# Graph layer with 512 columns: 16 gathered tiles per block and a loop of single tiles in place of 17 gathered tiles

## The reference

```
def _gin_conv(h, src, dst, w, b, eps, n_nodes):
    agg = jax.ops.segment_sum(h[src], dst, num_segments=n_nodes)
    return ((1.0 + eps) * h + agg) @ w + b
...
h = jax.nn.relu(_gin_conv(x, src, dst, w1, b1, eps1, n))
h = jax.nn.relu(_gin_conv(h, src, dst, w2, b2, eps2, n))
return _gin_conv(h, src, dst, w3, b3, eps3, n)
```

## Time and profile before

| | us |
|---|---|
| median of 3 runs | 4946.31 (4939.7 to 4948.61) |
| the profiled execution, its time | 4950.88 |
| the profiled execution, span from first to last instruction | 4949.2 |
| of it: attention layer with its gathers, about 622 to 1980 | 1358 |
| first graph layer, about 2340 to 3130 | 790 |
| 512-wide layer, about 3130 to 4335 | 1205 |
| last graph layer, about 4335 to 4949 | 614 |

### The profile page before, as it was taken

The page is one execution under the profiler, slowest core; times in us unless marked ns, Lnnn a source line. Parts: engine busy times, 40 slices in busy tenths (PEclk is TensorE's granted clock), DMA queues, the critical chain, the costliest instruction groups (busy, mean ns, idle before and its releaser), DMA issues. The chain is left out here.

```text
span 4949.2 us, 70593 instructions
## 1 busy us (share of the span) xinstructions
PE 3788.6 (77%) x15851; PEld 2474.8 (50%) x15852; DVE 2212.0 (45%) x7809; ACT 1419.7 (29%) x2721; POOL 2665.5 (54%) x4165
## 2 busy tenths in 40 slices
PE   3886645555555555885899999688888888879999
PEld 1233334444444444775677777344444444467777
DVE  6996756666666666345111121222222223222222
ACT  3982222222222222235344444100000010033333
POOL 6780066666666665013544444366666666655554
PEclk9999967777777777985999999899999999899999
DMA  4442133333333333026767666477777676656665
GB/s 137 174 190 68 55 93 90 88 92 92 93 89 93 93 93 81 0 59 176 200 186 203 190 183 180 148 207 212 207 210 209 206 213 204 183 167 188 200 183 170
DMA packets 347068, 730.73 MB, mean 148 GB/s; under 512 B 77999, under 2 KB 171821, under 8 KB 342577
## 3 DMA queue, kind: packets, MB, share of 16 engines
q0 software_dynamic: 176144, 461.72, 33.3%
q10 hardware_dynamic: 100802, 157.63, 10.2%
q1 hardware_dynamic: 69980, 109.80, 6.5%
HBM read 622.28 MB, written 106.64 MB: 147 GB/s over the span
## 5 line engine op out<-in xcount | busy, mean ns | idle before, releaser
L901 POOL DMA_INDIRECT a_gathered<-table,record x850 | 807.2, 950 | 688.0 <-issue 368.3
L2265 POOL DMA_INDIRECT l_gathered<-table,record x782 | 760.5, 972 | 478.2 <-issue 275.5
L2455 PE MATMUL bank<-l_gathered,l_onehot 128*125 128x512 f32 x1564 | 774.8, 649 | 189.5 <-DMA l_gathered<-table,record 108.0
L1829 POOL DMA_INDIRECT l_gathered<-table,record x578 | 546.6, 946 | 487.8 <-PE bank L2037 218.4
L1250 PE MATMUL bank<-a_gathered,a_onehot 128*125 128x264 f32 x1700 | 564.4, 490 | 101.0 <-DVE a_gathered L1054 85.6
L2455 PEld LDWEIGHTS bank<-l_gathered,l_onehot 128*125 128x125 f32 x1564 | 312.5, 205 | 629.8 <-issue 464.7
L1943 ACT ACTIVATE l_part<-l_packed 128x1000 fp32r<-128x1000 bf16 (+1 forms) x396 | 411.6, 1070 | 578.6 <-DMA l_packed<-adjacency 176.6
L1250 PEld LDWEIGHTS bank<-a_gathered,a_onehot 128*125 128x125 f32 x1700 | 389.3, 241 | 201.9 <-issue 67.5
L2018 PE MATMUL bank<-rows_last,l_part 125*125 125x512 f32 x1650 | 407.4, 404 | 35.1 <-ACT l_part L1943 22.4
L2018 PE MATMUL bank<-rows_first,l_part 125*125 125x512 f32 x1650 | 407.3, 406 | 35.1 <-ACT l_part L1943 35.1
L2018 PEld LDWEIGHTS bank<-rows_first,l_part 125*125 125x125 f32 x1650 | 309.0, 188 | 127.1 <-issue 44.6
(11 more groups left out here) (282 smaller groups left out, 5613.4 us busy)
## 6 DMA issues: line engine op xcount, KB each, us to landing
l_packed<-adjacency ACTq DMA_DIRECT2D x264, 250.0 KB
adjacency<-d_stage SPq DMA_DIRECT2D x33, 1562.5 KB
l_packed<-adjacency ACTq DMA_DIRECT2D x132, 281.2 KB
l_gathered<-table,record POOLq DMA_INDIRECT x1360
a_gathered<-table,record POOLq DMA_INDIRECT x850
table<-rows_first POOLq DMA_DIRECT2D x50, 250.0 KB, 3.4
table<-l_work ACTq DMA_DIRECT2D x50, 250.0 KB
l_source_rows<-table ACTq DMA_DIRECT2D x50, 250.0 KB
```

Source lines behind the costliest of these rows:

```text
L901: pool.indirect_dma_start(out=gathered0[s][:, j * TW:(j + 1) * TW], out_offset=None, in_=table0, in_offset=bass.IndirectOffsetOnAxis(ap=re ...
L1829: pool.indirect_dma_start(out=gathered[g][:, j, :], out_offset=None, in_=table, in_offset=bass.IndirectOffsetOnAxis(ap=record[k.t][:, j, 0 ...
L2265: pool.indirect_dma_start(out=gathered[:, j * w:(j + 1) * w], out_offset=None, in_=table, in_offset=bass.IndirectOffsetOnAxis(ap=record[t] ...
L2455: last = pe.matmul(total[0:NB, 0:w], onehot[t][:, j, :], rows[:, j, :], start=False, stop=(j == T - 1), skip_group_check=True)
```

## The change

A gathered block's first 2048 edges are now one fixed round of 16 tiles (`WT` = 16, `RW` = 2048), without a loop around it: record loads, gathers, one-hots and matmuls are plain code, and their waits count by the place in the order (`round_of`, `filled_of`). Edges from `rest_from[b]` = min(first_edge[b] + 2048, first_edge[b+1]) up to the block's end are single tiles of 128 edges, in a loop `Fori(lo, hi, P)` that usually runs no time. It is the loop that the tabled blocks already had, with a step of 128 in place of 32, and now serves both kinds. Its records are loaded by GpSimd (`gather_rest`) instead of SP. VectorE does its part of that loop at the end of the step (`onehot_rest`). PE starts the sum with its first tile instead of a matmul with zeros, and reads the bounds of the loop after the 16 tiles. Three small VectorE operations at the layer's start make `rest_from`, and GpSimd and PE wait for them.

The diff, cut to its core:

```
+WT = 16
+RW = WT * P
...
-                QUARTERS = [(0, 4), (4, 8), (8, 12), (12, T)]
+                QUARTERS = [(0, 4), (4, 8), (8, 12), (12, WT)]
...
-                onehot = tiles("onehot", [P, T, NB])
-                gathered = phase.enter_context(nc.sbuf_tensor(f"l{n}_gathered", [P, T * w], F32))[:, :]
+                onehot = tiles("onehot", [P, WT, NB])
+                gathered = phase.enter_context(nc.sbuf_tensor(f"l{n}_gathered", [P, WT * w], F32))[:, :]
...
+                def round_of(s, i):
+
+                    if isinstance(i, int) and i >= PAIRS - TABLED:
+                        return (PAIRS - TABLED) + (i - (PAIRS - TABLED)) // 2
+                    return i
+
+                def filled_of(s, i):
+
+                    if isinstance(i, int) and i >= PAIRS - TABLED:
+                        return 2 * (PAIRS - TABLED) + (i - (PAIRS - TABLED))
+                    return 2 * i + s
...
-                        ends = [first_edge[0:1, bass.ds(b + e, 1)] for e in range(2)]
+                        ends = [rest_from[0:1, bass.ds(b, 1)], first_edge[0:1, bass.ds(b + 1, 1)]]
...
+                def load_records(engine, s, i):
+                    if tabled(s, i):
+                        return
+                    t, r = record_of(s, i), round_of(s, i)
+                    lo = engine.value_load(first_edge[0:1, bass.ds(block_at(s, i), 1)], min_val=0, max_val=E)
+                    engine.wait_ge(round_gathered[t], r + 1)
+                    engine.dma_start(record[t][:, 0:WT, :].rearrange("p j c -> p (j c)"),
+                                     edges[bass.ds(lo, RW), :].rearrange("(p j) c -> p (j c)", j=WT)).then_inc(record_loaded[t], 16)
...
-                    def gather_few(lo, hi):
-                        with pool.Fori(lo, hi, OV) as at:
+                    def gather_rest():
+                        lo, hi = [pool.snap(reg, min_val=0, max_val=E) for reg in bounds]
+                        with pool.Fori(lo, hi, P) as at:
                             before = few_of(pool, few)
+                            wait_apart(pool, few_used, before + 1, 1)
+                            pool.dma_start(few_record[:, :], edges[bass.ds(at, P), :]).then_inc(few_loaded, 16)
                             wait_apart(pool, few_loaded, before * 16 + 16, 16)
                             pool.indirect_dma_start(
...
-                        with pool.Fori(lo, hi, RE) as at:
-                            wait_apart(pool, record_loaded[t], count_of(pool, rounds[t]) * 16 + 16, 16)
-                            before = count_of(pool, filled)
-                            for q, (j0, j1) in enumerate(QUARTERS):
...
+                        wait_apart(pool, record_loaded[t], round_of(s, i) * 16 + 16, 16)
+                        for q, (j0, j1) in enumerate(QUARTERS):
+
+                            wait_apart(pool, quarters_used, filled_of(s, i) * NQ + q + 1, 1)
+                            for j in range(j0, j1):
...
+                        gather_rest()
                         keep(found)
...
+                    dve.tensor_copy(first_f[:, :], first_edge[:, :]).then_inc(rest_steps, 1)
...
+                    dve.scalar_tensor_tensor(rest_f[:, :], first_f[:, 0:BLOCKS], float(RW), first_f[:, 1:BLOCKS + 1],
+                                             ALU.add, ALU.min).then_inc(rest_steps, 1)
...
+                    dve.tensor_copy(rest_from[:, :], rest_f[:, :]).then_inc(rest_ready, 1)
...
-                    over_steps(dve, [(rounds_of, 0), (finish, 1), (halve, 4)], split_source, 6, AHEAD + 1)
+                    over_steps(dve, [(onehots, 0), (finish, 1), (halve, 4), (onehot_rest, 0)], split_source, 6, AHEAD + 1)
...
-                            pe.matmul(total[0:NB, 0:w], zeros[:, 0:NB], zeros[:, 0:w], start=True, stop=True)
...
+                                    last = pe.matmul(total[0:NB, 0:w], onehot[t][:, j, :], rows[:, j, :], start=(j == 0),
+                                                     stop=False, skip_group_check=True)
...
+                        lo, hi = rest_range(pe, s, i)
+                        with pe.Fori(lo, hi, P) as at:
+                            before = few_of(pe, few)
+                            pe.wait_ge(few_ready, before + 1)
+                            pe.wait_ge(few_gathered, before * 16 + 16)
+                            pe.matmul(total[0:NB, 0:w], few_onehot[:, :], few_rows[:, :], start=False, stop=False,
+                                      skip_group_check=True).then_inc(few_used, 1)
+                            pe.reg_add(few, few, 1)
```

More of the change, by code:

```diff
@@ L2279, in _ @@
                 def _(dve):
-                    rounds, seen, used = counters(dve, "dve_r"), counters(dve, "dve_s"), counter(dve, "dve_g")
                     for s in range(2):
@@ L2286, in _, with onehots, onehot_rest @@
                     few = counter(dve, "dve_f")
-                    def onehot_few(s, i, lo, hi):
-                        with dve.Fori(lo, hi, OV) as at:
+                    dve.tensor_copy(first_f[:, :], first_edge[:, :]).then_inc(rest_steps, 1)
+                    dve.wait_ge(rest_steps, 1)
+                    dve.scalar_tensor_tensor(rest_f[:, :], first_f[:, 0:BLOCKS], float(RW), first_f[:, 1:BLOCKS + 1],
+                                             ALU.add, ALU.min).then_inc(rest_steps, 1)
+                    dve.wait_ge(rest_steps, 2)
+                    dve.tensor_copy(rest_from[:, :], rest_f[:, :]).then_inc(rest_ready, 1)
+                    dve.wait_ge(rest_ready, 1)
+                    def onehots(s, i):
+                        if tabled(s, i):
+                            return
+                        t, r = record_of(s, i), round_of(s, i)
+                        dve.wait_ge(record_loaded[t], r * 16 + 16)
+                        dve.tensor_scalar(relative[t][:, 0:WT], record[t][:, 0:WT, 1].bitcast(F32),
+                                          minus_base[:, bass.ds(block_at(s, i), 1)], None, ALU.add).then_inc(relative_ready[t], 1)
+                        dve.wait_ge(relative_ready[t], r + 1)
+                        if not isinstance(i, int) or filled_of(s, i) > 0:
+                            dve.wait_ge(quarters_used, filled_of(s, i) * NQ)
+                        for j in range(WT):
+                            last = dve.tensor_scalar(onehot[t][:, j, :], column[:, 0:NB], relative[t][:, j:j + 1], None, ALU.is_equal)
+                        last.then_inc(onehot_ready[t], 1)
+                    def onehot_rest(s, i):
+                        lo, hi = rest_range(dve, s, i)
+                        with dve.Fori(lo, hi, P) as at:
                             before = few_of(dve, few)
@@ L2430, in _, with sums @@
                         pe.sem_inc(source_used[r], 1)
-                    def rounds_of(s, i):
+                    pe.wait_ge(rest_ready, 1)
+                    def sums(s, i):
                         rows = gathered.rearrange("p (j c) -> p j c", c=w)
                         total = total_of(s, i)
-                        lo, hi = edge_range(pe, s, i)
-                        if tabled(s, i):
-                            with pe.Fori(lo, hi, OV) as at:
-                                before = few_of(pe, few)
-                                pe.wait_ge(few_ready, before + 1)
-                                pe.wait_ge(few_gathered, before * 16 + 16)
-                                pe.matmul(total[0:NB, 0:w], few_onehot[:, :], few_rows[:, :], start=False, stop=False,
-                                          skip_group_check=True).then_inc(few_used, 1)
-                                pe.reg_add(few, few, 1)
-                        else:
+                        if not tabled(s, i):
@@ L2445, in rounds_of @@
                             t = record_of(s, i)
                             pe.wait_ge(sums_read[s], i + 1)
-                            pe.matmul(total[0:NB, 0:w], zeros[:, 0:NB], zeros[:, 0:w], start=True, stop=True)
-                            with pe.Fori(lo, hi, RE) as at:
-                                pe.wait_ge(onehot_ready[t], count_of(pe, rounds[t]) + 1)
-                                before = count_of(pe, emptied)
-                                for q, (j0, j1) in enumerate(QUARTERS):
-                                    pe.wait_ge(rows_gathered[q], (before + 1) * (16 * (j1 - j0)))
-                                    for j in range(j0, j1):
-                                        last = pe.matmul(total[0:NB, 0:w], onehot[t][:, j, :], rows[:, j, :], start=False,
-                                                         stop=(j == T - 1), skip_group_check=True)
-                                        if j == T - 2:
-                                            last.then_inc(round_gathered[t], 1)
-                                    last.then_inc(quarters_used, 1)
-                                pe.reg_add(rounds[t], rounds[t], 1)
-                                pe.reg_add(emptied, emptied, 1)
@@ new lines, in sums @@
```

(9 more changed lines are left out.)

97 lines of the change are left out of this document (28 added, 69 removed).

## The result

| us | before | after |
|---|---|---|
| median | 4943.01 (4925.16 to 4948.61, 4 runs) | 4988.6 (4975.71 to 4998.77, 4 runs) |
| the profiled execution, span | 4949.2 | 4974.2 |
| 512-wide layer, first gather to the next layer's first | 1218.2 | 1273.4 |

The ratio is 1.0086, 95% interval 1.0044 to 1.0129: the change made the kernel 0.9% slower. The prediction was 4917, range 4888 to 4962. The layer lost 55.2 us. The parts before and after it came out 14.4 and 15.8 us shorter in this one execution, though nothing in them was changed, so its span rose by 25.0 only; the layer's own figure is the one to explain.

The account below looks back on a forecast made before the run. The prediction took GpSimd's time per gather to bound the 512-wide layer; -49 (plain periods) - 1.8 (ends) + 10 (single tiles) + 1 (tabled) + 11 (second wait) = -29 us, giving 4917 us, range 4888 to 4962.

Parts of the forecast that it names:

- What bounds the kernel: 512-wide layer: each block takes GpSimd a fixed time tied to its number of gathers, 1.40 us per gather.
- Is the 3.73 us a wait for PE?: GpSimd's idle time at a block boundary: answered no, as PE had finished the earlier block's first quarter 13 us before.
- So 46 tiles go and 6 single tiles come: Gathered blocks: each loses one tile, only six blocks above 2048 edges get a single tile; four tabled blocks keep theirs.
- the -49 us for 35 plain periods: Blocks without single tiles: 35 gather periods shrink by 1.40 us each, bounds -44 and -54.
- A period with a single tile: GpSimd stands for its own record load: 27.2 us against 25.24, five such periods +10 us, bounds +1 and +19.
- The second wait on the single buffer: Between blocks 46 and 47 GpSimd's load waits for PE to use the tile: 38 us against 26.8, +11.
- The last tabled block: After the last gathered block: its record and rows lie under PE's last 17.35 us, 0 or some 4 us.
- What hides the rest of the edit: PE's zeroing matmul and register loads, DVE's loads and start operations, SyncE's record loads: all this costs 0.
- Rival 1: Plain periods are held by PE's release and rows landing, staying 25.24 us: +22, 4968, slower; chance 0.13.
- PE bound: PE becomes the bound as its clock falls in gaps: 0.7 us less gain in 35 periods, about 4941; chance 0.08.
- the boundary that goes with the loop: Boundary idle time goes with the loop around the round, 4.4 us less in 35 periods: about -134, 4812; chance 0.04.
- The dearer single tile: Landing 5.5 us and full boundary of 4.9 each time, 31.1 us a period: +2, 4948, no change; chance 0.14.

Follow-up runs that it names:

- e3: The changed kernel with 17 fixed tiles a block and no single-tile loop in gathered blocks, against the kernel before: 4685.88 us, ratio 1.0012.
- e6: The changed kernel with 15 fixed tiles, no single tiles in gathered blocks, edges beyond 1920 left out, against the kernel before: 4766.63 us, ratio 0.9751.
- e5_guard_sp: The changed kernel with a test hi > lo around the single-tile loop and SyncE loading its records, against the kernel before: 4859.59 us, ratio 0.9921.
- e1b_guard: The changed kernel with a test hi > lo around the single-tile loop, GpSimd still loading, third chip, against the kernel before: 4868.83 us, ratio 0.9937.
- b2_before: The kernel before, unedited, traced on the second chip: 4887.02 us in its one run.

## Why the prediction was wrong, by its own steps

1. **What bounds the kernel: right in how the period moves, wrong in what the boundary is.** GpSimd's list sets the layer's time, and its period falls with the count of gathers: 17, 16 and 15 tiles gave 24.91, 23.56 and 22.10 us, 1.35 and 1.46 apart (predicted 1.40, bounds 1.25 and 1.53). Where the boundary idle is missing it is 1.13, under the lower bound. "Is the 3.73 us a wait for PE?" was answered no, by a matmul that had ended 13 us earlier. It is one: the update came at 3634.95. The term came out right all the same, because the update comes some 3 us after a block's last gather whether the block has 17, 16 or 15. The prediction did not know that, so this part was luck.
2. **"So 46 tiles go and 6 single tiles come": the step that failed.** 46 came. The counting of edges was right, but I read a loop whose ends are equal as no turn; it makes one. The sign was there: four single tiles in four tabled blocks, 66 in 66 in the trace of before, and, in the attention layer's code, a test `If(hi > lo + RE)` around just such a loop. Even "the four tabled blocks keep their one each" counted four needless turns as real. With this step wrong the -49 us for 35 plain periods was never there.
3. **A period with a single tile**: predicted 27.2 (25.4 to 29.0) against 25.24. The mean of the 40 after was 25.74, near the low bound. The load cost what I took: from its start to the start of the gather that waits for it 4.17 us in the median (3.59 to 6.88) for 3.4 + 0.7. Too much was the middle between 1.25 and 4.9 for what follows: the next block's first gather started 1.34 us after the single one in the mean, because the stand for the record had already taken the boundary's place. On the chip without boundary idle a real single tile cost 6.5.
4. **The second wait on the single buffer**: the mechanism was right, the number of places wrong. Predicted one period near 38; measured three of 35.6 to 36.0, because all neighbours of a tabled block have a tile now: +27.3 for predicted +11 and +1.
5. **The last tabled block, "0, or some 4 us if PE is done sooner"**: the tail grew by 8.7. The needless tile of the last gathered block holds the buffer until PE has used it, and only then is the load issued (4360.00). I had not carried the second wait to this place.
6. **What hides the rest of the edit: 0.** It held: in e3, the new code with 17 tiles, the ratio was 1.0012 [1.0003, 1.0021].
7. **The rivals.** None had the cause. Rival 1 forecast 4968 by a plain period of 25.2 and would have passed on that row alone (25.6 in the median after). It had right what ends the boundary's idle time, a release of PE; it had wrong that 16 tiles would take as long as 17, for they took 23.56 once the needless ones were gone. PE bound is refuted by e6, and the boundary that goes with the loop by e5_guard_sp, whose boundary idle is still there without it. The dearer single tile was true only of the chip without boundary idle.

With one turn in each block the prediction's own terms would have given: 46 gathers less and 46 more, 0; 40 plain periods at the low bound of 25.4, +6 (measured +19.8); three of 38, +34 (measured +27.3); tail +4 (measured +8.7). That is +44 against 55.2. The low bound is chosen here with the result known; with the middle that the prediction took, 27.2, the 40 periods alone make +78. The sign would have been right either way.

With the premise given back, six single tiles and no more, the measured ratio was 0.9937 [0.9913, 0.9962] (e1b_guard); the sum of -29 us makes 0.994. That it is so close is in part luck: the tabled places and the tail lost what no term has, 141.3 us there against 111.2 in b2_before.

The Trainium skill says in "DMA: Bandwidth & Descriptors", under the anatomy of a DMA on the gpsimd path, that one has a fixed cost of about 2.0 us. The traces have no landing of the 2 KB record loads. GpSimd's gather starts 2.61 us after such a load at least and 4.17 in the median, its wake-up included, so no run here shows that cost by itself.

## What to carry to other kernels

Read how often a run-time loop runs from the trace's counts, not from its source: a count that equals the number of visits where the data call for none is a body that always runs once, and a test `If(hi > lo)` around it is worth as much as the body and its waits. Here the changed kernel was 0.9 and 1.0% slower without it, and with it alone 0.6% faster on a chip of that kind (0.5% on the first chip, where the changed kernel was not run as it is). Applied to the same loop in all three graph layers, with SyncE's loads, it gave -2.0%, the fastest version tried that leaves no edge out.

A wait costs nothing as long as it falls into idle time that is there anyway: the same load by GpSimd cost next to nothing beside a boundary idle of 3.5 us, and a real single tile 6.5 us a block without one. "The matmul had ended long before" does not show that a wait was for something else: look for the semaphore's update, and see whether idle time that an edit seems to leave alone has moved. With a single buffer, ask for each pair of neighbours who uses it last, and look at the end of the stage as well.

## What the runs showed of the hardware

The same kernel took 4680 us on one chip, and 4882 to 4943 on others. Two thirds of the difference show in the wide layer: 1070.5 us in e3_17_fixed on the first chip, 1203.9 in b2_before. On the first the gathers followed each other with 0.30 us between them across the blocks' ends (21.55 us for 17, 1.27 each); elsewhere they did so within a block, and 3.1 to 4.2 us of idle time stood at its end, 3.8 in the median before, 3.4 with 16 tiles and 3.3 with 15. That idle time is the wait for an update of a semaphore that came 0.76 us before the next gather and up to 13.2 us after the end of the matmul that carries it, where on the first chip it came within 0.1 us. Whether GpSimd's row of gathers holds the updates up is not shown; that they came some 3 us after its last one is.

The Trainium skill says in "Perfetto Trace Analysis", on the DMA instruction of GpSimd, that the profiler shows it as ended when the last descriptor is written and not when the data have moved. No run here shows that directly.
